# Probability codes as bytes in fp16's 1024, with the 1024 taken off by the matrix engine

## Chip, cores and metric

One NeuronCore of a Trainium2 chip runs the whole program in one launch. The metric is the device time of one execution in microseconds; the time before is the median of three runs.

## What is computed

Four transformer blocks in a row on x [4, 512, 128] with a context [4, 154, 128], 16 heads of 8 in the first three. Only the third block's two attentions, which are fake-quantised, are touched here. One is self-attention (512 keys), one cross-attention (154 keys):

```python
def _fq(x, delta, zp, n_bits):
    xi = _round_ste(x / delta) + zp
    xq = jnp.clip(xi, 0.0, 2.0 ** n_bits - 1.0)
    return (xq - zp) * delta

sim = jnp.einsum('bhid,bhjd->bhij', _fq(q, dq, 128.0, 8), _fq(k, dk, 128.0, 8)) * SCALE
attn = jax.nn.softmax(sim, axis=-1)
out = jnp.einsum('bhij,bhjd->bhid', _fq(attn, dw, 0.0, 8), _fq(v, dv, 128.0, 8))
```

The probabilities become integer codes from 0 to 255 (probability / dw, rounded, clipped), the values integer codes from -128 to 127, and the products of codes are summed exactly.

## The kernel before, in words

Each engine runs a program of its own, written out by hand in the order of a table of items, and the engines meet at semaphores. A unit is one attention of one sequence; units 16 to 19 are the quantised self-attentions of the four sequences, 20 to 23 the cross-attentions. A unit is cut into steps: in self-attention 32, each of one tile of 128 queries with 2 heads and 512 keys; in cross-attention 16, each of one tile with 4 heads and 154 keys. That makes 192 steps. Two steps are a pair, 96 in all.

A step i goes through the engines like this (names as in the code):

- PE, `scores_quant(i)` (L1280): products of query and key codes into one of three double banks (`score0`, `score1`, `trans`); it waits until ACT is done with the bank's earlier step i-3.
- DVE, L2064: the largest score of every row (`top_score`). Ahead of it in DVE's loop stands the reciprocal L2058 of the row sums of step i-2 (in cross-attention L2057 scales them first).
- ACT, L1572 scales the tops, L1581 takes exp into `probs` (three slots) with the row sum `total`.
- POOL, L2278 (self-attention only) multiplies two reciprocals by 1/dw; L2289 makes the codes: probability times reciprocal plus 1024.0 (`HALF_ROUND`), written as fp16. Between 1024 and 2048 fp16 holds just the integers, so the write rounds. It is 2 instructions of 512 columns in a self-attention step and 4 of 154 in a cross-attention step, into `codes` (four slots).
- SP, L926: a DMA transpose of the step's [128, 1024] fp16 codes into `pT_raised` (eight slots).
- DVE, `copy_codes` (L2047): takes 1024 off, cuts at 255 and writes bf16 `pT_codes`; it runs `QUANT_LAG` = 6 steps behind DVE's top. `pT_codes` and `pT_raised` are one place in SBUF.
- PE, `weigh_pair(n)` (L1299): 16 products of value codes and probability codes, four of them in each of PE's column groups, summed into `acc`; it runs `WEIGH_LAG` = 8 steps behind.

After a unit's last pair DVE scales `acc` into `oT` (L2072). Among the steps the items of the neighbouring units run: output product and statistics (W), normalisation (M), transposed features (H), and the next unit's Q, K and V with their rounding on DVE. In units 16 and 17 POOL also issues 16 gathers of expert rows (L2235). Ahead of the stage stands the expert stage, whose last products end with semaphore `down_raised`; its buffers share SBUF with `codes`.

Elsewhere in the kernel, and used below as rows only: L2182, a POOL cast of 154 columns; L2188, a POOL multiplication of 154 bf16 columns by one column (`term_row`), with no second operation; L2189, a POOL sum of two bf16 operands; L2244, a POOL memset; L1246, the experts' down products.

Of the kernel before, what the change touches and what calls it, by code (L numbers as in the profile page):

```python
# [14 lines left out]
ROUND = 1.5 * 2.0 ** 23  # L15
HALF_ROUND = 1024.0
LOWEST = -1.0e30
# [5 lines left out]
CODE_SOURCES = 4  # L23
QUANT_LAG, WEIGH_LAG, GROUPED_LAG = 6, 8, 2

# [377 lines left out]
def build(nc, io, out):  # L403
# [3 lines left out]
    with ctx:  # L407
# [143 lines left out]
        put = place(arena, quant_at)  # L551
        k_codes = put([P, 2, TOKENS], bf16)
        quant_at = [16384]
        put = place(arena, quant_at)
        qT_codes, k4_codes = put([P, 2, TOKENS], bf16), put([P, 2, 4, TOKENS], bf16)

        v_quant, v_quant_tail = put([P, 2, TILES, HEADS, 32], bf16), put([P, 2, HEADS, 32], bf16)
        probs = put([P, 3, 2, TOKENS])
        pT_at = quant_at[0]
        pT_codes = put([P, CODE_SLOTS, 2 * TILES, P], bf16)  # L560
        put = place(arena, [pT_at])
        pT_raised = put([P, CODE_SLOTS, 2 * TILES, P], fp16)
        put = place(arena, [0])
        codes = put([P, CODE_SOURCES, 2, TOKENS], fp16)
        put = place(arena, quant_at)
        q_round, k_round, v_round = put([P, TOKENS]), put([P, TOKENS]), put([P, TILES, D])
# [108 lines left out]
        codes_ready = sem("codes_ready")  # L675
        codes_copied = sem("codes_copied")
        pair_weighed = sem("pair_weighed")
# [116 lines left out]
        with nc.Block() as block:  # L794

            @block.sync
            def _(sp):
# [122 lines left out]
                for i in range(len(QUANT_STEPS)):  # L920
                    if i in KEYS_AFTER:
                        copy_keys(KEYS_AFTER[i])
                    sp.wait_ge(codes_ready, i + 1)
                    if i >= CODE_SLOTS:
                        sp.wait_ge(pair_weighed, (i - CODE_SLOTS) // 2 + 1)
                    sp.dma_start_transpose(pT_raised[:, i % CODE_SLOTS, :, :],  # L926
                                           codes[:, i % CODE_SOURCES, :, :].rearrange("p j k -> p (j k)"))\
                        .then_inc(codes_turned[i % CODE_SLOTS], 16)
# [22 lines left out]
            def _(pe):  # L951
# [333 lines left out]
                def weigh_pair(n):  # L1285

                    u, t, _, first, heads = quant_step(2 * n)
                    pe.wait_ge(codes_copied, 2 * n + 2)
                    if 2 * n == QUANT_BASE[u]:
                        pe.wait_ge(v_coded, u - 15)  # L1290
                        if u > 16:
                            pe.wait_ge(oT_ready, u - 16)
                    tiles = 2 if is_cross(u) else TILES
                    for z in range(heads):
                        i = first + z
                        for k in range(tiles):
                            vals = v_quant_tail[:, u % 2, :, :] if is_cross(u) and k else v_quant[:, u % 2, k, :, :]
                            for j in range(4):
                                ins = nc.tensor.matmul(acc[32 * j:32 * j + 32, P * t:P * (t + 1)], vals[:, 4 * j + i, :],  # L1299
                                                       pT_codes[:, (2 * n + j // 2) % CODE_SLOTS, j % 2 * TILES + tiles * z + k, :],  # L1300
                                                       start=(i == 0 and k == 0), stop=(i == 3 and k == tiles - 1))
                    ins.then_inc(pair_weighed, 1)
# [41 lines left out]

                pe.wait_ge(codes_copied, len(QUANT_STEPS))
                pe.wait_ge(quant_exp, len(QUANT_STEPS))
# [295 lines left out]
            def _(dve):  # L1642
# [399 lines left out]

                def copy_codes(i):

                    of = i % CODE_SLOTS
                    dve.wait_ge(codes_turned[of], 16 * (i // CODE_SLOTS + 1))
                    nc.vector.tensor_scalar(pT_codes[:, of, :, :].rearrange("p k q -> p (k q)"),  # L2047
                                            pT_raised[:, of, :, :].rearrange("p k q -> p (k q)"),
                                            -HALF_ROUND, 255.0, ALU.add, ALU.min).then_inc(codes_copied, 1)

                quant_steps = len(QUANT_STEPS)
                for i in range(quant_steps + WEIGH_LAG + 2):
# [6 lines left out]
                    if i < quant_steps:  # L2059
                        src = quant_score[i % 3][:, :, :]  # L2060
                        if is_cross(QUANT_STEPS[i][0]):
# [3 lines left out]
                                                negate=True).then_inc(quant_top, 1)  # L2065
                    if QUANT_LAG <= i < quant_steps + QUANT_LAG:
                        copy_codes(i - QUANT_LAG)
                    if i in QUANT_LAST:
# [75 lines left out]
            def _(pool):  # L2144
# [121 lines left out]
                def of_step(z, i):  # L2266
                    u, t, a, h, heads = quant_step(i)
                    z = z[:, :].rearrange("p (t x j i) -> p t x j i", x=2, j=2, i=4)[:, t, a, :, h:h + heads]
                    return z if heads > 1 else z.rearrange("p j i -> p (j i)")

                quant_steps = len(QUANT_STEPS)
                for i in range(quant_steps + 1):
                    if i:
# [9 lines left out]
                        for j in range(2):  # L2283
                            for z in range(heads):
# [3 lines left out]
                                to = slice(z * 2 * P, z * 2 * P + width)  # L2288
                                ins = nc.gpsimd.tensor_scalar(codes[:, (i - 1) % CODE_SOURCES, j, to], probs[:, (i - 1) % 3, j, of],  # L2289
                                                              inv_total[:, at_col:at_col + 1], HALF_ROUND, ALU.mult, ALU.add)  # L2290
                        ins.then_inc(codes_ready, 1)
# [99 lines left out]
```

## Time and profile before

| | |
|---|---|
| median of 3 runs | 1576.75 us (1573.37 to 1578.98) |
| the profiled execution | 1576.92 us |
| its span | 1575.1 us |
| mean granted clock of PE | 0.826 |
| PE busy | 1092.8 us |
| DVE busy | 1098.1 us |
| ACT busy | 894.2 us |
| POOL busy | 681.1 us |

Busy times are sums over the whole span. The quantised stage begins at about 685 us and ends at about 1167 us. A "wait" is idle time of an engine put down to what released it; a clock of 0.50 is the lower of PE's two levels, 1.2 GHz.

### The profile page before, as it was taken

The page shows a single profiled execution, that of the slowest core. Times are in us where ns is not written, and L with a number is a line of the kernel's source. Part 1 is how long each engine was busy: PE and PEld are TensorE (multiplying, and loading weights), DVE is VectorE, ACT ScalarE, POOL GpSimd, SP SyncE. Part 2 cuts the span into 40 slices and gives each one's busy share as a digit, 9 for nine tenths or more (in the row PEclk, how much of TensorE's full clock was granted, in tenths as well). Part 3 has the DMA queues.
Part 4 walks back from the last instruction along what each step waited for, and adds up shares of the span by engine and source line. Part 5 has one row for each costly group of instructions (what it writes and reads, how often), then busy time and mean ns, then how long its engine had stood idle before and what let it go on. Part 6 is the DMA issues. An engine that isn't in the chain of part 4 may idle for free.

```text
span 1575.1 us, 28607 instructions
## 1 busy us (share of the span) xinstructions
PE 1092.8 (69%) x9344; PEld 593.3 (38%) x9344; DVE 1098.1 (70%) x3102; ACT 894.2 (57%) x2546; POOL 681.1 (43%) x1055
## 2 busy tenths in 40 slices
PE   2888888887788797855353545444358778888888
PEld 1333344444333286831120212222225435453545
DVE  2687777777688653678888999877765666666522
ACT  1555554555554464567676797988852344646531
POOL 3321011011011416558888888877741344445310
PEclk9899999999999998975555555555569799999989
DMA  5213142101331112267555576665530121201000
GB/s 184 61 53 92 51 129 75 54 24 50 99 106 49 42 39 82 57 160 122 99 104 109 106 130 115 121 109 106 109 57 14 27 48 35 49 21 43 1 0 27
DMA packets 265219, 116.53 MB, mean 74 GB/s; under 512 B 216936, under 2 KB 253936, under 8 KB 262896
## 3 DMA queue, kind: packets, MB, share of 16 engines
q1 hardware_dynamic: 260112, 108.29, 30.8%
q0 software_dynamic: 2048, 4.20, 0.9%
q10 hardware_dynamic: 2912, 2.22, 0.5%
q8 instruction: 75, 1.23, 0.3%
q14 instruction: 72, 0.59, 0.1%
HBM read 38.80 MB, written 16.45 MB: 35 GB/s over the span
## 4 chain that ended last, share of the span: by engine, by line
PE 35%; POOL 21%; DVE 18%; issue 14%; ACT 9%; DMA 1%; SPq 0%; POOLq 0%; another core or an unknown queue 0%; ACTq 0%; DVEq 0%
POOL arena L2289 12%; ACT arena L1581 4%; PE acc L1199 3%; POOL inv_total L2278 2%; PE trans L1171 2%; DVE minus_top L1980 2%; PE misc L1021 2%; PE misc L1027 2%; PE trans L1323 2%; ACT arena L1528 2%; PE score L1335 2%; PE score L1337 2%; PE trans L1177 1%; POOL arena L2235 1%; PE acc L1385 1%
## 5 line engine op out<-in xcount | busy, mean ns | idle before, releaser
L2289 POOL TENSOR_SCALAR arena<-arena,inv_total 128x512 f16<-128x512 f32 (+1 forms) x512 | 299.7, 585 | 57.3 <-DVE inv_total L2058 16.8
L1980 DVE TENSOR_REDUCE minus_top<-score 128x4 f32<-128x616 f32 (+4 forms) x256 | 200.6, 802 | 95.3 <-PE score L1141 36.9
L2154 POOL TENSOR_TENSOR rstd<-spread,minus_half 128x4 f32<-128x4 f32 x36 | 37.5, 1043 | 489.5 <-DVE spread L1662 414.0
L1581 ACT ACTIVATE arena<-score,minus_top,exp_scale 128x512 f32<-128x512 f32 (+1 forms) x340 | 210.4, 625 | 20.9 <-POOL arena L2289 11.9
L1528 ACT ACTIVATE arena<-trans 128x512 f32<-128x512 f32 x240 | 134.4, 596 | 109.3 <-PE trans L1177 104.0
L1619 ACT ACTIVATE arena<-arena,minus_top 128x154 f32<-128x154 f32 x256 | 105.2, 412 | 129.3 <-DVE minus_top L2123 129.1
L1280 PE MATMUL score<-arena 32*128 32x512 bf16 (+1 forms) x340 | 68.9, 458 | 139.7 <-ACT arena L1581 138.7
L2064 DVE TENSOR_REDUCE top_score<-score 128x2 f32<-128x1024 f32 (+1 forms) x128 | 135.7, 1061 | 0.6 <-PE score L1280 0.5
L2309 POOL TENSOR_TENSOR arena<-arena,inv_total 128x512 f32<-128x512 f32 x64 | 66.5, 1040 | 143.9 <-DVE inv_total L2131 130.0
L1581 ACT ACTIVATE arena<-trans,minus_top,exp_scale 128x154 f32<-128x154 f32 (+1 forms) x172 | 105.5, 620 | 19.2 <-POOL arena L2289 14.9
L2118 DVE CUSTOM_DVE_ANT_0 arena<-score,arena 128x154 f32<-128x154 f32 x256 | 65.9, 313 | 60.6 <-PE score L1360 60.2
L2047 DVE TENSOR_SCALAR arena<-arena 128x1024 bf16<-128x1024 f16 x192 | 103.1, 537 | 5.9 <-DMA arena<-arena 5.9
L1572 ACT ACTIVATE minus_top<-top_score,exp_scale 128x2 f32<-128x2 f32 (+1 forms) x192 | 56.4, 294 | 52.9 <-DVE top_score L2064 52.4
L1280 PEld LDWEIGHTS score<-arena 32*128 32x128 bf16 x340 | 14.2, 102 | 191.0 <-ACT arena L1581 173.9
L1280 PE MATMUL trans<-arena 32*128 32x154 bf16 (+1 forms) x172 | 34.9, 454 | 72.8 <-ACT arena L1581 72.8
L1199 PE MATMUL acc<-arena 128*32 128x512 f32 (+3 forms) x768 | 79.9, 504 | 4.7 <-issue 4.0
L1299 PE MATMUL acc<-arena 128*32 128x128 bf16 x1536 | 59.3, 307 | 27.9 <-DVE oT L2072 15.3
L1546 ACT ACTIVATE arena<-score,arena 128x128 f32<-128x128 f32 x184 | 52.0, 370 | 44.2 <-PE score L1236 38.1
L1528 ACT ACTIVATE arena<-trans,arena 128x512 f32<-128x512 f32 x80 | 52.2, 686 | 28.5 <-PE trans L1177 27.3
L2064 DVE TENSOR_REDUCE top_score<-trans 128x2 f32<-128x1024 f32 (+1 forms) x64 | 67.4, 1053 | 0.0
L1581 ACT ACTIVATION_READ_ACCUMULATOR arena<-score,minus_top,exp_scale 128x1 f32 x340 | 66.6, 196 | 0.0
L1177 PE MATMUL trans<-arena 64*128 64x512 bf16 (+3 forms) x384 | 63.3, 327 | 0.0
(283 smaller groups left out, 2814.4 us busy)
## 6 DMA issues: line engine op xcount, KB each, us to landing
arena<-q_terms SPq DMA_DIRECT2D x88, 128.0 KB, 2.8
late<-arena SPq DMA_DIRECT2D x128, 64.0 KB, 2.0
q_terms<-arena SPq DMA_DIRECT2D x36, 128.0 KB
late<-k_terms SPq DMA_DIRECT2D x32, 128.0 KB, 3.1
arena<-arena SPq DMA_TRANSPOSE x192, 3.1
by_expert<-zeros SPq DMA_DIRECT2D x2, 1472.0 KB, 9.8
arena<-by_expert SPq DMA_DIRECT2D x10, 256.0 KB
from_expert<-arena SPq DMA_DIRECT2D x10, 256.0 KB
```

Source lines behind the costliest of these rows:

```text
L1177: ins = nc.tensor.matmul(to, ones[r, j, :], top_rows[r, g % 2, q0:TOKENS], start=False, stop=True)
L1199: ins = nc.tensor.matmul(acc[32 * j:32 * j + 32, q0:TOKENS], v_cols[:, k, 4 * g + j, :], src, start=(b % half == 0 and k == 0), stop=(last ...
L1280: ins = nc.tensor.matmul(quant_score[i % 3][:, j, z * n:(z + 1) * n], qT_codes[r:r + 32, u % 2, t * P:(t + 1) * P], k4_codes[r:r + 32, u % ...
L1528: nc.scalar.activation(expT[w % SLOTS], trans[w % 2][:, :], ACT.Exp, bias=bias)\
L1581: ins = nc.scalar.activation(probs[:, i % 3, j, of], quant_score[i % 3][:, j, of], ACT.Exp, bias=minus_top[:, at_col:at_col + 1], scale=ex ...
L1619: ins = nc.scalar.activation(gq_exp_p[:, i % 3, h, :], shifted[:, i % 3, h, :], ACT.Exp, bias=minus_top[:, at_col:at_col + 1], accum_out=t ...
L1980: nc.vector.tensor_reduce(dst, src, axis=AX.X, op=ALU.max, negate=True).then_inc(top_ready, 1)
L2047: nc.vector.tensor_scalar(pT_codes[:, of, :, :].rearrange("p k q -> p (k q)"), pT_raised[:, of, :, :].rearrange("p k q -> p (k q)"), -HALF ...
L2064: nc.vector.tensor_reduce(of_step(top_score, i), src, axis=AX.X, op=ALU.max, negate=True).then_inc(quant_top, 1)
L2118: ins = nc.vector.tensor_tensor_reduce(out=shifted[:, i % 3, h, :], in0=score[i % 2][:, odd, z * CTX:(z + 1) * CTX], in1=mask_add[:, b % 2 ...
L2289: ins = nc.gpsimd.tensor_scalar(codes[:, (i - 1) % CODE_SOURCES, j, to], probs[:, (i - 1) % 3, j, of], inv_total[:, at_col:at_col + 1], HA ...
L2309: nc.gpsimd.tensor_tensor(gq_p[:, v % 2, :, :], gq_exp_p[:, v % 3, :, 0:P], inv.to_broadcast([P, 4, P]), ALU.mult)
```

## The change

`codes` is filled once with 1024.0, and a constant tile `minus_base` of -1024.0 is made. POOL's L2289 now only multiplies, and writes its result as unsigned bytes into the low byte of each fp16 code, so that the fp16 reads 1024 + code. The DMA transpose writes straight into `pT_codes`, which is fp16 now, as are the value codes. DVE's `copy_codes` is gone. PE's `weigh_pair` waits for the transposes, and follows each four products by four more of the same values with `minus_base`, which take off 1024 times the values' sum. Semaphore `codes_set` takes the place of `codes_copied`.

```diff
-        v_quant, v_quant_tail = put([P, 2, TILES, HEADS, 32], bf16), put([P, 2, HEADS, 32], bf16)
+        v_quant, v_quant_tail = put([P, 2, TILES, HEADS, 32], fp16), put([P, 2, HEADS, 32], fp16)
...
+        pT_codes = put([P, CODE_SLOTS, 2 * TILES, P], fp16)
         put = place(arena, [0])
+
         codes = put([P, CODE_SOURCES, 2, TOKENS], fp16)
+        code_bytes = codes.rearrange("p i j k -> p (i j k)").bitcast(mybir.dt.uint8)
+        code_bytes = code_bytes.rearrange("p (i j k b) -> p i j k b", i=CODE_SOURCES, j=2, b=2)[:, :, :, :, 0]
...
                 def weigh_pair(n):
 
                     u, t, _, first, heads = quant_step(2 * n)
-                    pe.wait_ge(codes_copied, 2 * n + 2)
+                    for i in (2 * n, 2 * n + 1):
+                        pe.wait_ge(codes_turned[i % CODE_SLOTS], 16 * (i // CODE_SLOTS + 1))
...
                             for j in range(4):
-                                ins = nc.tensor.matmul(acc[32 * j:32 * j + 32, P * t:P * (t + 1)], vals[:, 4 * j + i, :],
-                                                       pT_codes[:, (2 * n + j // 2) % CODE_SLOTS, j % 2 * TILES + tiles * z + k, :],
-                                                       start=(i == 0 and k == 0), stop=(i == 3 and k == tiles - 1))
+                                nc.tensor.matmul(acc[32 * j:32 * j + 32, P * t:P * (t + 1)], vals[:, 4 * j + i, :],
+                                                 pT_codes[:, (2 * n + j // 2) % CODE_SLOTS, j % 2 * TILES + tiles * z + k, :],
+                                                 start=(i == 0 and k == 0), stop=False)
+                            for j in range(4):
+                                ins = nc.tensor.matmul(acc[32 * j:32 * j + 32, P * t:P * (t + 1)], vals[:, 4 * j + i, :], minus_base,
+                                                       start=False, stop=(i == 3 and k == tiles - 1))
...
-                def copy_codes(i):
-
-                    of = i % CODE_SLOTS
-                    dve.wait_ge(codes_turned[of], 16 * (i // CODE_SLOTS + 1))
-                    nc.vector.tensor_scalar(pT_codes[:, of, :, :].rearrange("p k q -> p (k q)"),
-                                            pT_raised[:, of, :, :].rearrange("p k q -> p (k q)"),
-                                            -HALF_ROUND, 255.0, ALU.add, ALU.min).then_inc(codes_copied, 1)
...
+                pool.wait_ge(down_raised, ALL_BLOCKS)
+                nc.gpsimd.memset(codes.rearrange("p i j k -> p (i j k)"), CODE_BASE).then_inc(codes_set, 1)
+                nc.gpsimd.memset(minus_base, -CODE_BASE).then_inc(codes_set, 1)
+                pool.wait_ge(codes_set, 2)
...
-                                ins = nc.gpsimd.tensor_scalar(codes[:, (i - 1) % CODE_SOURCES, j, to], probs[:, (i - 1) % 3, j, of],
-                                                              inv_total[:, at_col:at_col + 1], HALF_ROUND, ALU.mult, ALU.add)
+
+                                ins = nc.gpsimd.tensor_scalar(code_bytes[:, (i - 1) % CODE_SOURCES, j, to], probs[:, (i - 1) % 3, j, of],
+                                                              inv_total[:, at_col:at_col + 1], None, ALU.mult)
```

On DVE, in the middle of unit 16, the order before was this (L2047 the copy, L2058 the reciprocal, L2064 the tops):

```order
L2058 RECIPROCAL inv_total<-total 128x2
L2064 TENSOR_REDUCE top_score<-score1 128x2
L2047 TENSOR_SCALAR arena<-arena 128x1024
L2058 RECIPROCAL inv_total<-total 128x2
L2064 TENSOR_REDUCE top_score<-trans 128x2
```

and is now this (L2053 and L2059 are the same two lines of the changed file):

```order
L2053 RECIPROCAL inv_total<-total 128x2
L2059 TENSOR_REDUCE top_score<-score0 128x2
L2053 RECIPROCAL inv_total<-total 128x2
L2059 TENSOR_REDUCE top_score<-score1 128x2
L2053 RECIPROCAL inv_total<-total 128x2
```

The third instruction of every step has gone; nothing else on DVE changes place.

On POOL, where the stage begins, the order is now this (L2276 and L2288 are the lines that were L2278 and L2289):

```order
L2151 TENSOR_TENSOR x<-x,rows 128x512
L2266 MEMSET arena 128x4096
L2267 MEMSET arena 128x128
L2276 TENSOR_SCALAR inv_total<-inv_total,inv_sizes 128x2
L2288 TENSOR_SCALAR arena<-arena,inv_total 128x512 x2
```

The two fills stand between the expert stage's last item and the first step's multiplication; before, the multiplication followed directly.

On PE a pair was one row, sixteen L1299 between the scores of two steps:

```order
L1280 MATMUL trans<-arena 128x512 x2
L1280 MATMUL score<-arena 128x512 x2
L1299 MATMUL acc<-arena 32x128 x16
L1280 MATMUL score<-arena 128x512 x2
L1280 MATMUL trans<-arena 128x512 x2
```

and begins now like this, with the two rows of four repeated four times for each pair:

```order
L1280 MATMUL trans<-arena 128x512 x2
L1280 MATMUL score<-arena 128x512 x2
L1300 MATMUL acc<-arena 32x128 x4
L1304 MATMUL acc<-arena 32x128 x4
L1300 MATMUL acc<-arena 32x128 x4
```

The scores keep their place; a pair has 32 matmuls where it had 16.

## Rows read from the trace of the kernel before

**Rows 1.** The page, busy us (share of the span), instructions.

```profile
PE 1092.8 (69%) x9344; PEld 593.3 (38%) x9344; DVE 1098.1 (70%) x3102; ACT 894.2 (57%) x2546; POOL 681.1 (43%) x1055
```

**Rows 2.** Busy time by unit; columns in the first row; units 17 and 21.

```profile
core 0: us, PE busy (x) PEld busy (x) DVE busy (x) ACT busy (x) POOL busy (x), PEclk, DMA share, GB/s
...
788.00:875.00 87.00, 37.48 (x348) 14.90 (x348) 75.92 (x158) 61.40 (x166) 74.53 (x114) 0.50 0.58 107
...
1059.00:1099.00 40.00, 18.36 (x212) 9.12 (x212) 31.05 (x98) 35.06 (x145) 30.92 (x67) 0.50 0.55 106
```

**Rows 3.** Timeline of POOL at the stage's start (start, duration, then idle before).

```profile
690.56 0.31 POOL L2278 TENSOR_SCALAR inv_total<-inv_total,inv_sizes 128x2 f32<-128x2 f32 x1 [8.97 <-DVE inv_total L2058]
...
692.51 0.29 POOL L2278 TENSOR_SCALAR inv_total<-inv_total,inv_sizes 128x2 f32<-128x2 f32 x1
...
694.44 0.29 POOL L2278 TENSOR_SCALAR inv_total<-inv_total,inv_sizes 128x2 f32<-128x2 f32 x1
```

**Rows 4.** Timeline of POOL, later in self-attention.

```profile
922.08 0.34 POOL L2278 TENSOR_SCALAR inv_total<-inv_total,inv_sizes 128x2 f32<-128x2 f32 x1
...
924.07 0.34 POOL L2278 TENSOR_SCALAR inv_total<-inv_total,inv_sizes 128x2 f32<-128x2 f32 x1
```

**Rows 5.** Timeline of all engines at the same place.

```profile
920.58 1.21 DVE L2064 TENSOR_REDUCE top_score<-score 128x2 f32<-128x1024 f32 x1
920.74 0.78 ACT L1581 ACTIVATE arena<-trans,minus_top,exp_scale 128x512 f32<-128x512 f32 x1
...
921.05 0.62 PE L1299 MATMUL acc<-arena 128*32 128x128 bf16 x16
...
922.64 0.78 ACT L1581 ACTIVATE arena<-score,minus_top,exp_scale 128x512 f32<-128x512 f32 x1
...
923.60 0.65 DVE L2047 TENSOR_SCALAR arena<-arena 128x1024 bf16<-128x1024 f16 x1
```

**Rows 6.** Waits from 700 to 1167: us in total, times, longest us.

```profile
PE score L1280 <- ACT arena L1581: 130.5, 88, 5.2
...
ACT minus_top L1572 <- DVE top_score L2064: 49.8, 35, 3.8
...
ACT arena L1581 <- POOL arena L2289: 26.8, 48, 1.6
...
POOL arena L2289 <- DVE inv_total L2058: 16.8, 21, 2.6
POOL inv_total L2278 <- DVE inv_total L2058: 11.4, 11, 2.1
```

**Rows 7.** DVE's groups, 690 to 1170: busy us, mean ns, idle before.

```profile
L2047 DVE TENSOR_SCALAR arena<-arena 128x1024 bf16<-128x1024 f16 x192 | 103.1, 537 | 5.9 <-DMA arena<-arena 5.9
```

**Rows 8.** POOL's groups over the span, by shape.

```profile
L2289 POOL TENSOR_SCALAR arena<-arena,inv_total 128x512 f16<-128x512 f32 x256 | 184.6, 721 | 22.4 <-DMA arena<-arena 1.1
L2289 POOL TENSOR_SCALAR arena<-arena,inv_total 128x154 f16<-128x154 f32 x256 | 115.1, 450 | 34.9 <-DVE inv_total L2058 16.8
...
L2278 POOL TENSOR_SCALAR inv_total<-inv_total,inv_sizes 128x2 f32<-128x2 f32 x128 | 43.2, 338 | 29.4 <-DVE inv_total L2058 20.3
...
L2188 POOL TENSOR_SCALAR arena<-arena,term_row 128x154 bf16<-128x154 bf16 x12 | 8.3, 691 | 1.2
...
L2244 POOL MEMSET arena<- 128x2048 f32 x1 | 1.8, 1818 | 0.0
...
L2189 POOL TENSOR_TENSOR arena<-arena 128x154 bf16<-128x154 bf16 x4 | 1.8, 444 | 0.3
...
L2182 POOL CAST arena<-arena 128x154 bf16<-128x154 f32 x4 | 1.2, 312 | 0.3
```

**Rows 9.** Single lines: ns min/median/max, starts; L2289 before 699 only.

```profile
L2188 POOL TENSOR_SCALAR arena<-arena,term_row x12: 674/675/817, 12.7 to 112.2; 128x154 bf16<-128x154 bf16 x12
...
L2289 POOL TENSOR_SCALAR arena<-arena,inv_total x8: 692/692/692, 691.0 to 697.5; 128x512 f16<-128x512 f32 x8
```

**Rows 10.** The chain of waits: start, us, what; the last expert.

```profile
683.50 1.07 PE trans L1246 x8
```

More of the change, by code:

```diff
@@ L15 @@
 ROUND = 1.5 * 2.0 ** 23
-HALF_ROUND = 1024.0
+CODE_BASE = 1024.0
 LOWEST = -1.0e30
@@ L23 @@
 CODE_SOURCES = 4
-QUANT_LAG, WEIGH_LAG, GROUPED_LAG = 6, 8, 2
+WEIGH_LAG, GROUPED_LAG = 8, 2
 PAIR_TILES = 2 * TILES
@@ L551, in build @@
         put = place(arena, quant_at)
-        k_codes = put([P, 2, TOKENS], bf16)
+        k_codes, minus_base = put([P, 2, TOKENS], bf16), put([P, P], fp16)
         quant_at = [16384]
@@ L555, in build @@
         qT_codes, k4_codes = put([P, 2, TOKENS], bf16), put([P, 2, 4, TOKENS], bf16)
-        v_quant, v_quant_tail = put([P, 2, TILES, HEADS, 32], bf16), put([P, 2, HEADS, 32], bf16)
+        v_quant, v_quant_tail = put([P, 2, TILES, HEADS, 32], fp16), put([P, 2, HEADS, 32], fp16)
         probs = put([P, 3, 2, TOKENS])
[L559 to L562, printed above, removed]
+        pT_codes = put([P, CODE_SLOTS, 2 * TILES, P], fp16)
         put = place(arena, [0])
         codes = put([P, CODE_SOURCES, 2, TOKENS], fp16)
+        code_bytes = codes.rearrange("p i j k -> p (i j k)").bitcast(mybir.dt.uint8)
+        code_bytes = code_bytes.rearrange("p (i j k b) -> p i j k b", i=CODE_SOURCES, j=2, b=2)[:, :, :, :, 0]
         put = place(arena, quant_at)
@@ L675, in build @@
         codes_ready = sem("codes_ready")
-        codes_copied = sem("codes_copied")
+        codes_set = sem("codes_set")
         pair_weighed = sem("pair_weighed")
@@ L925, in _ @@
                         sp.wait_ge(pair_weighed, (i - CODE_SLOTS) // 2 + 1)
-                    sp.dma_start_transpose(pT_raised[:, i % CODE_SLOTS, :, :],
+                    sp.dma_start_transpose(pT_codes[:, i % CODE_SLOTS, :, :],
                                            codes[:, i % CODE_SOURCES, :, :].rearrange("p j k -> p (j k)"))\
@@ L1343, in feed_forward @@
                     downs(B - 1)
-                pe.wait_ge(codes_copied, len(QUANT_STEPS))
                 pe.wait_ge(quant_exp, len(QUANT_STEPS))
@@ L2065, in _ @@
                                                 negate=True).then_inc(quant_top, 1)
-                    if QUANT_LAG <= i < quant_steps + QUANT_LAG:
-                        copy_codes(i - QUANT_LAG)
                     if i in QUANT_LAST:
```

## The prediction

> **What bounds the kernel now.** The page's busy shares come first [rows 1]: the busiest, DVE, works 70% of the span, and the average over stages says little: the stage of the change has to be read alone. That is the two quantised attentions, units 16 to 23, from 690.5 to 1166.7 us of the span. Its busy time by unit [rows 2] shows how near three engines are to their limit: in unit 17, self-attention, DVE works 75.92, ACT 61.40 and POOL 74.53 of 87.00 us; in unit 21, cross, ACT leads with 35.06 of 40.00. PE works under half the time, at a granted clock of 0.50 (its lower level, 1.2 GHz).
>
> Which of the three ends last is read from the timeline of POOL. In the first steps, before the first L2047 runs on DVE, a POOL step repeats every 1.95 and 1.93 us: 690.56, 692.51, 694.44 [rows 3]. Later it starts at 922.08 and 924.07, 1.99 us apart [rows 4], while ACT's steps start at 920.74 and 922.64, 1.90 apart [rows 5]. POOL is the slowest by 4%, ACT is next, and DVE (1.21 for the top and 0.65 for L2047 alone [rows 5]) has no slack to catch up when the Q, K, V and normalisation items come between. The waits confirm both [rows 6]: ACT waits 26.8 us for POOL's L2289 and 49.8 us for DVE's tops; POOL waits 16.8 + 11.4 us for DVE's reciprocals. PE's long waits are for ACT, 130.5 us on the score banks: it has spare time.
>
> **Removed from DVE.** 192 copies L2047, 103.1 us [rows 7]: 0.54 us a step. It lies on no bound directly; it pays in two ways.
> (a) POOL runs freer. With L2047 present L2289 takes 721 ns in the mean over the 256 wide ones and L2278 338 [rows 8]; before the first L2047 they take 692 and 290 [rows 9, 3]. 256 x 0.029 + 128 x 0.048 = 7.4 + 6.1 = 13.5 us, all in self-attention and all on the bound.
> (b) POOL's 28.2 us of waiting for DVE [rows 6]. DVE gains 0.5 us a step to catch up, but the items themselves stay. Between none and all, I take half, 14 us: item work is larger than L2047 at any one place, yet L2047 is what keeps DVE late in the steps after it.
> The Trainium skill (SBUF — State Buffer, section "Who interferes with whom") says that a VectorE instruction in a 2-port mode, as a tensor_scalar within SBUF can be, blocks GpSimd fully. By that rule the 128 copies of the self-attentions, 0.54 us each, would have blocked POOL for up to 69 us. The rows show 13.5, so most copies must fall where POOL doesn't ask for the ports, or give way themselves; the sum goes by the rows.
>
> **Changed on POOL.** 512 L2289, each now one multiplication to bytes at every second place instead of a multiplication and an addition to fp16. No row shows a byte output. Lower bound: the 154-column cast L2182, 312 ns against 450 of the 154-column L2289 [rows 8], so 138 ns less. POOL would drop well under ACT, whose 1.90 us against POOL's 1.93 would bound: 128 x 0.03 = 4 us more gain in self-attention, and the other half of POOL's waits, 14 us. Upper bound: L2188, the only other POOL operation that multiplies by a column and does nothing else: 691 ns for 154 columns (median 675 [rows 9]), half again as much as L2289, with bf16 in and out. I take no change, from the row nearest in input, width and column scalar: L2289 itself. Why not L2188: its input is 16 bits wide, as the new one's is not. But the row speaks against the change and carries the main rival.
>
> **Start on POOL.** Two memsets, of 4096 and 128 fp16 columns, after the last expert. 2048 f32 columns take 1818 ns [rows 8]: by bytes the large one would take 1.8 us, by columns 3.64. I take 3.64, and under 0.3 for the small one. The last expert's L1246 ends at about 684.56, so they run from 684.7 to 688.7; POOL's first step starts at 690.56 after 8.97 us idle [rows 10, 3]. They cost nothing, with 1.9 us to spare; without that cover, 4 us once.
>
> **Added on PE.** 16 more matmuls a pair on the same operand shapes, with their weight loads. 16 take 0.62 us from the first start to the last end [rows 5], so 96 x 0.62 = 59.5 us of PE time at the low clock. The cover is PE's waiting for ACT, 130.5 us over the stage on the score banks alone [rows 6]; with three banks scores are also issued a step before DVE reads them, so 0.62 us of lateness every second step does not reach DVE. Where it isn't covered is the end of a unit: last pair, oT, output product. PE now waits for the transpose itself and not for the copy behind it, 0.54 us, so 0.1 net a unit; with PE's items near by I take +2 us in all. Bounds: 0 and 30 (half uncovered).
>
> **DMA** moves the same bytes in transposes of the same shape; only the place they land in has another type. Cost nothing.
>
> **Sum** against the profiled execution's 1576.9 us (span 1575.1; the median of the runs is 1576.75, the same): -13.5 - 14 + 2 = -25.5, rounded to **1552 us.** A measurement of this kernel tells from no change about 0.3%, 4.7 us; 25 is well beyond that.
>
> **Rivals.**
> *B, slower: the one-operation byte form is slow on POOL.* L2188's excess over L2289 is 0.225 us on 154 columns (675 against 450). In proportion to columns that is 0.748 on 512. Self-attention: 256 x 0.748 = 191.5 us; cross: 256 x 0.225 = 57.6. POOL is then the bound everywhere, so its waits and contention are swallowed: 191.5 + 57.6 - 28.2 - 13.5 = +207.4, **1784 us**; read as slope over a fixed 0.29 (0.385 us for 152 columns), the wide one would take 1.58 us, the excess 0.89, and the time 1821. For it: L2188 takes 674 to 817 ns in all 12 places, so it is no collision; and bf16 alone is slow neither as input (L2189, a sum of two bf16 operands, 444 ns) nor as output (L2182) [rows 8, 9]. Against: two stages of arithmetic being cheaper than one needs a path made for just that pair; L2278, also one multiplication, is as cheap as it can be, but has two columns. It turns the sign already when the wide form costs over 0.1 us more: 256 x 0.1 = 26 us.
> The Trainium skill (GPSIMD Engine Reference, sections 3.1 and 4.1) speaks for the forecast: it calls one-input work roughly line-rate and bound by the port up to two operations an element; by it the new form would cost what the old one did, and the forecast stands as it is. L2188 doesn't fit that rule.
>
> *C, PE's additions show.* If half of the 59.5 us lands on the path (scores late behind the longer pair, then tops, then ACT), -27.5 + 30 = +2.5: **1579 us**, no change. For: at the end of a unit PE items and the pair stand in a row. Against: 130.5 us of waiting for ACT.
>
> *D, ACT bounds.* POOL's byte form is cheaper, as the cast's row allows, and DVE's lateness vanishes with its copies: ACT's 1.90 us a step and none of POOL's 28 us of waits: -13.5 - 28 - 4 + 2 = -43.5, **1533 us**. For: ACT has the longest steady busy time in cross units [rows 2]. Against: DVE's items are still there.
>
> *E, the change doesn't do what it says*: the slowdown of L2289 isn't from L2047, POOL stays at 1.99 and only DVE frees itself: -14 + 2, **1565 us**. Still faster.
>
> **How the numbers follow.** Forecast (with E) 0.48, D 0.08, C 0.08, B 0.36. The gain needs one thing only, an unchanged L2289, and the one row that is like its new form speaks against; hence 0.36 and no less. Faster by over 0.3% 0.56, within 0.3% 0.08, slower 0.36. The forecast's own range is 1538 to 1567. The range of all reaches from 1535 over C to 1800, which takes in B in proportion and leaves out its steeper form and D.
>
> **What would show it.** In the profile after: no DVE line for copies, DVE near 64% of the span ((1098.1 - 103.1)/1552); the POOL group of codes at 690 ns (forecast) or over 1.3 us (B) for 512 columns; the small POOL multiplication back at 290 ns; a POOL step of 1.93 us; ACT's wait for DVE's tops well under 49.8 us; POOL's memset over by 688.6; a pair's 32 matmuls in 1.24 us at clock 0.50. I am wrong if codes cost over 0.1 us more, if PE's matmuls of pairs become what DVE's tops wait for, or if POOL steps in 1.93 us and the stage is no shorter.

## Result: 12.6% slower, and the profile after

The changed kernel takes 1775.06 us in the median of 4 runs (1763.69 to 1780.65), the kernel before 1575.06 in the runs beside it (4 runs). The ratio is 1.126, 95% interval 1.119 to 1.133: slower by some 200 us. The forecast of 1552 was wrong, rival B (1784) was what happened, and the time lies inside the range of all, 1535 to 1800. The profiled execution took 1763.69 us, its span is 1761.9.

The page's busy row of the kernel after answers to [rows 1]:

```profile
PE 1125.5 (64%) x10880; PEld 630.4 (36%) x10880; DVE 1024.9 (58%) x2910; ACT 893.0 (51%) x2546; POOL 946.9 (54%) x1057
```

DVE lost 73 us, ACT none; POOL gained 266. (DVE's 73 are less than the copies' 103.1 for two reasons: a copy started some 0.09 us before the top ahead of it ended, which the page counts once, 192 x 0.09 = 17 us; and DVE's other instructions in the stage got longer by 13 us in sum, 7.2 of them in L2052, the scaling of the cross-attentions.) Where POOL gained them is in its groups by shape (lines moved: L2289 is now L2288, L2278 is L2276), beside [rows 8]:

```profile
L2288 POOL TENSOR_SCALAR arena<-arena,inv_total 128x512 uint8<-128x512 f32 x256 | 399.8, 1574 | 11.9
L2288 POOL TENSOR_SCALAR arena<-arena,inv_total 128x154 uint8<-128x154 f32 x256 | 169.8, 703 | 0.4
...
L2276 POOL TENSOR_SCALAR inv_total<-inv_total,inv_sizes 128x2 f32<-128x2 f32 x128 | 39.5, 309 | 3.6 <-DVE inv_total L2053 2.2
```

A multiplication that used to take 721 ns takes 1574, the short one 703 instead of 450. POOL's waits for DVE have shrunk to almost nothing. The timeline of POOL at the stage's start, with the two fills, answers to [rows 3]:

```profile
685.44 3.51 POOL L2266 MEMSET arena<- 128x4096 f16 x1 [3.09 <-PE trans L1246]
688.89 0.21 POOL L2267 MEMSET arena<- 128x128 f16 x1
...
694.82 0.30 POOL L2276 TENSOR_SCALAR inv_total<-inv_total,inv_sizes 128x2 f32<-128x2 f32 x1
695.22 3.11 POOL L2288 TENSOR_SCALAR arena<-arena,inv_total 128x512 uint8<-128x512 f32 x2
698.29 0.30 POOL L2276 TENSOR_SCALAR inv_total<-inv_total,inv_sizes 128x2 f32<-128x2 f32 x1
```

The fills are over at 689.1, before the first step needs POOL. A step then repeats every 3.47 us instead of 1.93. The waits from 700 to 1362 say who stands behind POOL, beside [rows 6]:

```profile
ACT arena L1584 <- POOL arena L2288: 250.9, 173, 3.2
PE score L1280 <- ACT arena L1584: 229.8, 99, 5.6
DVE inv_total L2053 <- ACT arena L1584: 204.4, 94, 3.5
...
ACT minus_top L1575 <- DVE top_score L2059: 30.7, 18, 3.7
```

The order of these is a chain: ACT waits 250.9 us (26.8 before) because `probs` has three slots and POOL has not read the oldest; PE and DVE wait for ACT. POOL alone waits for nobody. The busy time of the stage adds up; these are the windows before (684.5 to 1167) and after (685 to 1362):

```profile
684.50:1167.00 482.50, 211.70 (x2210) 89.35 (x2210) 401.36 (x923) 382.18 (x1227) 387.88 (x680) 0.51 0.63 117
```

```profile
685.00:1362.00 677.00, 252.33 (x3748) 129.70 (x3748) 328.24 (x731) 380.51 (x1228) 653.44 (x682) 0.52 0.44 84
```

POOL (the fifth engine of the row) worked 387.9 of 482.5 us and now works 653.4 of 677.0. Its work rose by 265.6, its idle time fell from 94.6 to 23.6, by 71.0: 265.6 - 71.0 = 194.6 us, the 194.5 by which the stage is longer. All of the loss is there and is POOL's.

### The profile page after: what moved, and what is told of

Same layout as the page of the kernel before. It is cut to its first block, busy times and chain, and to the rows that moved or that the text cites. A ratio compares the mean times of both kernels' runs of the same rounds, so it can differ in the third digit from the quotient of the medians.

```text
span 1761.9 us, 31585 instructions
## 1 busy us (share of the span) xinstructions
PE 1125.5 (64%) x10880; PEld 630.4 (36%) x10880; DVE 1024.9 (58%) x2910; ACT 893.0 (51%) x2546; POOL 946.9 (54%) x1057
## 4 chain that ended last, share of the span: by engine, by line
POOL 37%; PE 30%; DVE 14%; issue 12%; ACT 5%; DMA 1%; SPq 0%; POOLq 0%; DVEq 0%; ACTq 0%
POOL arena L2288 28%; PE acc L1199 2%; DVE minus_top L1983 2%; POOL inv_total L2276 2%; PE trans L1171 2%; PE misc L1021 2%; PE misc L1027 2%; PE trans L1327 2%; ACT arena L1531 2%; PE score L1339 1%; PE score L1341 1%; DVE arena L1749 1%; PE trans L1177 1%; POOL arena L2228 1%; PE score L1236 1%
## 5 line engine op out<-in xcount | busy, mean ns | idle before, releaser
L2288 POOL TENSOR_SCALAR arena<-arena,inv_total 128x512 uint8<-128x512 f32 (+1 forms) x512 | 569.5, 1139 | 12.3
L2053 DVE RECIPROCAL inv_total<-total 128x2 f32<-128x2 f32 (+1 forms) x192 | 32.8, 171 | 210.6 <-ACT arena L1584 208.3
L2059 DVE TENSOR_REDUCE top_score<-score 128x2 f32<-128x1024 f32 (+1 forms) x128 | 135.8, 1062 | 1.6 <-PE score L1280 1.6
L1300 PE MATMUL acc<-arena 128*32 128x128 f16 x1536 | 89.3, 306 | 25.1 <-DMA arena<-arena 13.3
L1304 PE MATMUL acc<-arena 128*32 128x128 f16 x1536 | 91.9, 312 | 0.0
L1300 PEld LDWEIGHTS acc<-arena 128*32 128x32 f16 x1536 | 54.3, 137 | 59.3 <-issue 59.1
L2059 DVE TENSOR_REDUCE top_score<-trans 128x2 f32<-128x1024 f32 (+1 forms) x64 | 67.5, 1055 | 0.5 <-PE trans L1280 0.5
L1531 ACT ACTIVATE arena<-trans,arena 128x512 f32<-128x512 f32 x80 | 52.3, 687 | 28.7 <-PE trans L1177 27.5
```

Of the source, the lines that this page charges most:

```text
L1531: nc.scalar.activation(expT[w % SLOTS], trans[w % 2][:, :], ACT.Exp, bias=bias)\
L2059: nc.vector.tensor_reduce(of_step(top_score, i), src, axis=AX.X, op=ALU.max, negate=True).then_inc(quant_top, 1)
L2288: ins = nc.gpsimd.tensor_scalar(code_bytes[:, (i - 1) % CODE_SOURCES, j, to], probs[:, (i - 1) % 3, j, of], inv_total[:, at_col:at_col + 1 ...
```

## The experiments

What in L2288 is slow? Three things about it are new: the byte output, its stride of two bytes, and the missing second operation. Theory 1 says it is the missing operation, theory 2 the bytes or their stride. Four kernels put this question and price PE's added products; four more divide the gain that is left once L2288 is mended.

Executions of one kernel differ by up to 19 us, and in the profiled ones much of that arises ahead of the stage: the first reciprocal starts anywhere from 690.2 to 705.1 us, behind code that no edit touches but e8's, and that in 12 short instructions. So two measures stand in this table: the ratio of whole times, with its interval, and the stage of the one profiled execution, from the first start of the reciprocal (L2058, now L2053) to the start of the last `oT` (L2072, now L2065).

| kernel | median us (runs) | ratio to before | stage us |
|---|---|---|---|
| before | 1576.75 (3) | | 690.2 to 1166.7: 476.5 |
| after | 1775.06 (4) | 1.126 [1.119, 1.133] | 691.0 to 1361.7: 670.7 |
| e1_two_ops_bytes | 1561.97 (4) | 0.988 [0.983, 0.993] | 705.1 to 1157.8: 452.7 |
| e2_one_op_fp16 | 1805.54 (1) | one execution, none taken | 700.5 to 1396.9: 696.4 |
| e4_pe_only | 1585.20 (10) | 1.004 [1.001, 1.007] | 692.8 to 1173.5: 480.7 |
| e5_no_take_off | 1558.93 (6) | 0.985 [0.981, 0.990] | 697.5 to 1147.3: 449.8 |
| e6_copy_back | 1579.14 (12) | 0.998 [0.995, 1.001] | 698.3 to 1170.1: 471.8 |
| e7_scale_in_second_op | 1548.14 (6) | 0.978 [0.975, 0.981] | 701.9 to 1145.1: 443.2 |
| e8_pads_two_ops | 1541.02 (5) | 0.980 [0.977, 0.982] | 692.0 to 1135.3: 443.3 |

The kernel before took 1582.4 to 1582.6 in the median beside e1 to e7, and 1576.5 beside e8; the ratios take that into account. How well the stage of one execution repeats is known from one pair only: e7 and e8 run the same instructions in it and took 443.2 and 443.3 us.

**e1_two_ops_bytes**: the changed kernel, with a second operation that does nothing.

```diff
-    inv_total[:, at_col:at_col + 1], None, ALU.mult)
+    inv_total[:, at_col:at_col + 1], 0.0, ALU.mult, ALU.add)
```

> The changed kernel with one word more: POOL's L2288 multiplies and adds 0.0, into the same bytes. Theory 1 (a tensor_scalar with a column and no second operation is slow on POOL, whatever it writes): L2288 falls from 1574 to about 690 ns (512 columns) and from 703 to about 450 ns (154), a POOL step of 1.93 us, and the whole to the forecast's 1552 us (1538 to 1567), faster than both kernels. Theory 2 (writing bytes at every second place is slow): L2288 stays near 1574 and 703 ns, the time near 1775 us. Theory 3 (both have a part): in between, about 1650 us.

Measured: ratio 0.988, where the change itself gave 1.126. POOL's groups in the stage:

```profile
L2288 POOL TENSOR_SCALAR arena<-arena,inv_total 128x512 uint8<-128x512 f32 x256 | 176.4, 702 | 14.2 <-DMA arena<-arena 2.3
L2288 POOL TENSOR_SCALAR arena<-arena,inv_total 128x154 uint8<-128x154 f32 x256 | 97.7, 406 | 50.6 <-DVE inv_total L2053 50.2
L2276 POOL TENSOR_SCALAR inv_total<-inv_total,inv_sizes 128x2 f32<-128x2 f32 x128 | 38.0, 297 | 28.7 <-DVE inv_total L2053 26.9
```

Adding 0.0 takes the instruction from 1574 to 702 ns, to the same byte places. The same change, with two operations, is faster than the kernel before.

**e2_one_op_fp16**: the other way round, the kernel before with its addition left out. The codes then lack the 1024, so the copies take off what isn't there and the attention sums are something else.

```diff
-    inv_total[:, at_col:at_col + 1], HALF_ROUND, ALU.mult, ALU.add)
+    inv_total[:, at_col:at_col + 1], None, ALU.mult)
```

> The kernel before with the addition of 1024 left out of L2289 (so the codes are not raised, and the copy on DVE takes 1024 off nothing: the quantised attentions compute something else). Theory 1: L2289 rises from 721 to about 1570 ns and from 450 to about 700, the time to about 1780 us. Theory 2: L2289 stays at 721 and 450 ns, and the time at 1575 us. Theory 3: in between.

POOL's groups, with no byte anywhere:

```profile
L2289 POOL TENSOR_SCALAR arena<-arena,inv_total 128x512 f16<-128x512 f32 x256 | 408.7, 1607 | 12.0
L2289 POOL TENSOR_SCALAR arena<-arena,inv_total 128x154 f16<-128x154 f32 x256 | 180.7, 725 | 0.4
```

The whole loss comes back without the rest of the change (1805.54 us in the one execution, where about 1780 was expected; DVE's copies are still there). Theory 2 has fallen.

**e3_pool_forms**: e1 with 57 POOL instructions behind the fills, on the experts' idle buffer, each form four times on 512 columns. They lengthen the kernel, to 1617.77 us in one execution, and touch nothing it reads.

```diff
+    for _ in range(4):
+        then(nc.gpsimd.tensor_scalar(h_out, f_in, col_s, 1024.0, ALU.mult, ALU.add))
+    for _ in range(4):
+        then(nc.gpsimd.tensor_scalar(h_out, f_in, col_s, None, ALU.mult))
...
```

> The two-operation byte kernel with 57 POOL instructions put behind the two fills, four of each form, each waiting for the one before, 512 columns each: multiplication by a column alone or with an addition, into fp16, f32, bytes side by side and bytes at every second place, bf16 to bf16, and with a number in place of the column, also two multiplications, and a cast to bytes. Theory 1: each form with one operation takes about 1.5 us and each with two 0.7, for every type. Theory 2: fp16 and f32 outputs take 0.7 us with either, byte outputs 1.5 us; if the stride matters, only the spread ones. A third possibility, that only a column as operand with one operation is slow, shows in the forms with a number. The time of the whole says nothing here: all engines wait for these instructions, some 60 us.

The forms by type, column as scalar (L2280 one operation with fp16 out, L2278 two; L2282 and L2284 the same with f32 out; L2286 bytes, one, L2288 two; L2290 bytes at every second place, one, L2292 two; L2294 bf16 in and out, one, L2296 two), then with a number in place of the column (L2298 one, L2300 two), and a cast:

```profile
L2280 POOL TENSOR_SCALAR arena<-arena,inv_sizes 128x512 f16<-128x512 f32 x4 | 6.3, 1566 | 0.4
...
L2290 POOL TENSOR_SCALAR arena<-arena,inv_sizes 128x512 uint8<-128x512 f32 x4 | 6.3, 1564 | 0.4
L2286 POOL TENSOR_SCALAR arena<-arena,inv_sizes 128x512 uint8<-128x512 f32 x4 | 6.2, 1562 | 0.4
L2282 POOL TENSOR_SCALAR arena<-arena,inv_sizes 128x512 f32<-128x512 f32 x4 | 6.2, 1562 | 0.4
L2294 POOL TENSOR_SCALAR arena<-arena,inv_sizes 128x512 bf16<-128x512 bf16 x4 | 6.2, 1562 | 0.4
L2298 POOL TENSOR_SCALAR arena<-arena 128x512 f16<-128x512 f32 x4 | 5.9, 1487 | 0.3
...
L2292 POOL TENSOR_SCALAR arena<-arena,inv_sizes 128x512 uint8<-128x512 f32 x4 | 2.8, 695 | 0.4
L2288 POOL TENSOR_SCALAR arena<-arena,inv_sizes 128x512 uint8<-128x512 f32 x4 | 2.8, 692 | 0.4
L2278 POOL TENSOR_SCALAR arena<-arena,inv_sizes 128x512 f16<-128x512 f32 x4 | 2.8, 692 | 0.4
L2284 POOL TENSOR_SCALAR arena<-arena,inv_sizes 128x512 f32<-128x512 f32 x4 | 2.8, 692 | 0.4
L2296 POOL TENSOR_SCALAR arena<-arena,inv_sizes 128x512 bf16<-128x512 bf16 x4 | 2.8, 692 | 0.4
...
L2300 POOL TENSOR_SCALAR arena<-arena 128x512 f16<-128x512 f32 x4 | 2.5, 617 | 0.3
L2304 POOL CAST arena<-arena 128x512 uint8<-128x512 f32 x4 | 2.4, 612 | 0.3
```

One operation costs 1562 to 1566 ns and two cost 692 to 695, whatever the types and the stride: 2.26 times as much. With a number it is 1487 against 617. The types, the bytes and the stride are worth 4 ns at most. The first operation is a multiplication in every form tried.

**e4_pe_only**: the kernel before with PE's added products alone, against a tile of zeros (`no_base`, bf16, filled once by POOL). The diff shows the added products.

```diff
+    for j in range(4):
+        ins = nc.tensor.matmul(acc[32 * j:32 * j + 32, P * t:P * (t + 1)], vals[:, 4 * j + i, :], no_base,
+                               start=False, stop=(i == 3 and k == tiles - 1))
```

> The kernel before with the 16 further products a pair added, by a tile of zeros in place of -1024, and nothing else changed (POOL fills the tile once). If PE's added 59.5 us lie under its waits for ACT, as I argued: no change, 1575 to 1580 us. If half of it shows (rival C): 1600 us or more.

Ratio 1.004, 6 us (1.7 to 10.4), and 4.2 us in the stage: small, though not the none that was expected. PE's wait for ACT covers nearly all of the added products. Rival C, which had half of them on the path, falls.

**e5_no_take_off**: e1 without the products with `minus_base`; the 1024s stay in the sums, so this kernel leaves the taking off out. The diff shows the products that are gone.

```diff
-    for j in range(4):
-        ins = nc.tensor.matmul(acc[32 * j:32 * j + 32, P * t:P * (t + 1)], vals[:, 4 * j + i, :], minus_base,
-                               start=False, stop=(i == 3 and k == tiles - 1))
```

> e1_two_ops_bytes without the products with minus_base: the 1024s stay in the sums, so the output is not the reference's. It prices PE's 96 x 0.62 = 59.5 us in the place where they stand, with DVE's copies gone. Theory (the waits for ACT cover them, as e4_pe_only showed on the kernel before, +6 us of 59.5): 2 to 8 us faster than e1_two_ops_bytes' ratio gives, ratio to the kernel before 0.983 to 0.987. Rival C in part (with DVE and POOL quicker, the longer pair is what delays the scores, and it ate what DVE's copies gave): 12 us or more faster than e1_two_ops_bytes, ratio 0.980 or less.

The ratio is 0.985 against e1's 0.988; their intervals overlap, so the runs don't tell them apart: by the ratios alone the difference could be anything from none to 14 us. The stage is 2.9 us shorter. It is the stage that puts the products' price in place at a few us, and the 12 of the rival didn't appear in it.

**e6_copy_back**: e1 with DVE's 192 copies put back into a tile that nobody reads, PE waiting for them (the lines that place the tile are not shown).

```diff
+    def copy_codes(i):
+        of = i % CODE_SLOTS
+        if i:
+            dve.wait_ge(codes_copied, i)
+        dve.wait_ge(codes_turned[of], 16 * (i // CODE_SLOTS + 1))
+        nc.vector.tensor_scalar(copied.rearrange("p k q -> p (k q)"), pT_codes[:, of, :, :].rearrange("p k q -> p (k q)"),
+                                -CODE_BASE, 255.0, ALU.add, ALU.min).then_inc(codes_copied, 1)
...
-    for i in (2 * n, 2 * n + 1):
-        pe.wait_ge(codes_turned[i % CODE_SLOTS], 16 * (i // CODE_SLOTS + 1))
+    pe.wait_ge(codes_copied, 2 * n + 2)
```

> e1_two_ops_bytes with DVE's copies put back, 192 of 512 columns as before, into a scratch tile that nobody reads, and PE waiting for the copy as before; the products with minus_base stay. Theory (the gain is DVE's: contention on POOL 13.5 us, and POOL's and ACT's waits for DVE): L2288 back from 702 to about 720 ns, the small POOL multiplication from 297 to about 338, and the time at the kernel before plus what PE adds, ratio 0.998 to 1.008. Rival (the gain comes from POOL's side, byte output or the two operations' form, or from PE not waiting for a copy): ratio at or under 0.993.

Ratio 0.998 (0.995 to 1.001): most of e1's gain goes; the stage is 19.1 us longer than e1's. So most of the gain is the copies', but not all of it. e6 has PE's added products as e4 has, and DVE's copies as well, and its stage is 8.9 us shorter than e4's (471.8 against 480.7; the ratios, 0.998 and 1.004, say the same). POOL's step is 1.89 us here with a copy in it (925.15 to 927.04), and was 1.99 before [rows 4]; what made it shorter is taken up below, under POOL's step. The timeline of DVE and then of POOL in mid-stage shows both engines paying (L2053 is the copy, L2301 the codes):

```profile
925.75 0.75 DVE L2053 TENSOR_SCALAR arena<-arena 128x1024 bf16<-128x1024 f16 x1
...
927.66 0.74 DVE L2053 TENSOR_SCALAR arena<-arena 128x1024 bf16<-128x1024 f16 x1
```

```profile
925.15 0.29 POOL L2289 TENSOR_SCALAR inv_total<-inv_total,inv_sizes 128x2 f32<-128x2 f32 x1
925.53 1.53 POOL L2301 TENSOR_SCALAR arena<-arena,inv_total 128x512 uint8<-128x512 f32 x2
927.04 0.29 POOL L2289 TENSOR_SCALAR inv_total<-inv_total,inv_sizes 128x2 f32<-128x2 f32 x1
```

The pair of codes takes 1.53 us beside a copy and 1.36 in e1, and the copy 0.75 (0.54 in the mean of [rows 7], but 0.42 in the median and 0.40 at the least, so about 0.42 where POOL leaves it alone):

```profile
L2047 DVE TENSOR_SCALAR arena<-arena x192: 395/424/1070, 699.6 to 1165.5; 128x1024 bf16<-128x1024 f16 x192
```

In the means of the groups the codes go from 702 to 757 ns (wide) and 406 to 447 (narrow), the small multiplication from 297 to 325: 256 x 0.055 + 256 x 0.041 + 128 x 0.028 = 28 us of POOL's work, where the forecast had 13.5. For the wide codes 720 ns were expected here, not 757.

**e7_scale_in_second_op**: e1 with work for the second operation. The scale goes into it, so POOL's small multiplication (L2276, in self-attention) and DVE's (L2052, in cross-attention) fall away.

```diff
-    then(nc.vector.tensor_scalar(t, t, sizes[:, 7:8], None, ALU.mult))
...
-    then(nc.gpsimd.tensor_scalar(of_step(inv_total, i - 1), of_step(inv_total, i - 1),
-                                 inv_sizes[:, 3:4], None, ALU.mult))
...
-    inv_total[:, at_col:at_col + 1], 0.0, ALU.mult, ALU.add)
+    inv_total[:, at_col:at_col + 1], inv_sizes[:, 7:8] if is_cross(u) else inv_sizes[:, 3:4], ALU.mult, ALU.mult)
```

> e1_two_ops_bytes with a use for the second operation: the codes are multiplied by the column 1/total and then by the column with the scale, so POOL's small multiplication of each self-attention step (297 ns) and DVE's of each cross step (L2052) fall away; the same values are computed. If POOL's step bounds the self-attentions: its step falls by 0.3 us to ACT's 1.90 at most, and half of POOL's 0.3 x 128 = 38 us shows, 8 to 20 us faster than e1_two_ops_bytes, ratio 0.975 to 0.983. If DVE with its items and ACT already bound there (POOL waits 77 us for DVE in e1_two_ops_bytes): under 5 us, ratio 0.985 to 0.988.

Ratio 0.978 (0.975 to 0.981), 15 us under e1 by the ratios, and the stage another 9.5 us shorter: the first of the two expectations. The codes' own rows are dearer, and POOL still has time left:

```profile
L2283 POOL TENSOR_SCALAR arena<-arena,inv_total,inv_sizes 128x512 uint8<-128x512 f32 x256 | 193.9, 769 | 54.6 <-DVE inv_total L2051 49.5 <-DMA arena<-arena 3.5
```

```profile
930.19 1.52 POOL L2283 TENSOR_SCALAR arena<-arena,inv_total,inv_sizes 128x512 uint8<-128x512 f32 x2 [0.38 <-DVE inv_total L2051]
932.10 1.52 POOL L2283 TENSOR_SCALAR arena<-arena,inv_total,inv_sizes 128x512 uint8<-128x512 f32 x2 [0.39 <-DVE inv_total L2051]
```

A second column costs 67 ns an instruction (769 against 702), 0.13 a step, and saves the small one's 0.30 and the gap of 0.10 behind it. POOL now idles 0.39 us of every 1.91. The starts of the eight `oT` divide the 9.5 us, since POOL's small multiplication stood only in the self-attentions and DVE's only in the cross-attentions: against e1 the four self-attentions are 7.2 us shorter (3.9, 2.5, 0.3 and 0.5), the four cross-attentions 2.3. So two thirds of the gain lie where POOL has the 16 gathers as well, in units 16 and 17; the steps of 1.91 us, the same in both kernels, give nothing.

**e8_pads_two_ops**: e7 with the same cure for the pads' multiplication, the row the prediction took for a warning (L2188 before, L2179 here).

```diff
-    pad_terms[:, t, :], pad_terms[:, t, :], term_row[:, t:t + 1], None, ALU.mult))
+    pad_terms[:, t, :], pad_terms[:, t, :], term_row[:, t:t + 1], 0.0, ALU.mult, ALU.add))
```

> e7_scale_in_second_op with the same cure for the row that the prediction read as a warning: POOL's 12 multiplications of the pad terms by a column (154 bf16 columns, median 674 ns) get an addition of 0.0 as second operation. Theory (any tensor_scalar on POOL without a second operation takes the slow form): from 674 to about 400 ns, near the 406 of the 154-column codes. Rival (bf16 or writing in place made that row slow): it stays at 674. The time: 12 x 0.27 = 3.3 us at most if POOL's pads were on a path, none if not; ratio 0.976 to 0.980.

The single line, to be read beside [rows 9]:

```profile
L2179 POOL TENSOR_SCALAR arena<-arena,term_row x12: 394/400/537, 12.8 to 111.2; 128x154 bf16<-128x154 bf16 x12
```

From a median of 675 ns to 400. That warning was the same effect, and nothing else. The time doesn't move (0.980 against 0.978, intervals overlapping; the stage 443.3 against 443.2): these 12 instructions are on no path. e7 and e8 are the fastest kernels of the study, about 33 us under the kernel before by their ratios.

## Why the prediction was wrong, and where it was right

**The step that failed** is "Changed on POOL ... I take no change, from the row nearest in input, width and column scalar". Nearness was judged by types and shape, and the types are worth 4 ns at most. What mattered was the form: how many operations the instruction carries. The one row of that form, L2188 at 675 ns for 154 columns [rows 9], was set aside because its input is bf16. e1 and e2 turn the effect off and on with that operand alone, e3 shows it for each type, and e8 cures L2188 itself. The argument against B, that two operations can't be cheaper than one without a path made for just that pair, is wrong: multiplication with addition and multiplication with multiplication (e7) are both fast. The runs don't show why. L2278, cheap with one operation, could say nothing on the question: by the prices per column worked out in the last section, its two columns carry 3 ns of the effect.

The rule of the Trainium skill (GPSIMD Engine Reference, sections 3.1 and 4.1) was weighed as speaking for the forecast: one-input work bound by the port up to two operations an element. By it the new form costs what the old did. The runs show 1562 against 692 ns, so for one operation without a second it doesn't hold here; the measurement decides.

**Rival B** gave 1784 for a measured 1775, by two errors that nearly cancel. Its operations were too small: 191.5 + 57.6 = 249.1 us against the groups' (399.8 - 184.6) + (169.8 - 115.1) = 269.9. Its cover was too small as well: 28.2 of waits and 13.5 of contention make 41.7, where POOL's idle time fell by 71.0 (the contention is in the groups' growth already). The waits named for DVE were not all of POOL's idle time; the difference between a stage's length and an engine's work in it is. What the forecast left out are mostly gaps of some 0.07 us that followed nearly every codes instruction of the kernel before, 36.5 us in all over 466 of them in its trace, and that the changed kernel hasn't (more under POOL's step). Its steeper reading, L2188 as a slope over a fixed part, gave 1.58 us for the wide form: 1574 ns measured. It missed by 46 us, two thirds through the same small cover, one third through its operations: 256 x 0.89 + 57.6 = 285.4 for the measured 269.9.

**The rest of the forecast**, read in e1, which is the change with POOL's form mended. Forecast was -25.5 us; the ratio says -19 (-11 to -27), the stage -23.8. That it comes so near is in part luck: by the stages it is +4.2 for PE (e4), -8.9 for what byte codes with 0.0 changed besides (e6 against e4; the gaps that POOL loses, below, are the likely part), which the forecast didn't have, and -19.1 for the copies (e1 against e6), where it had -27.5. By unit, from the starts of `oT`, 16.1 of the 23.8 us are in units 16 and 17, where POOL also issues the gathers, 3.5 in units 18 and 19, and 4.2 in the cross-attentions.
- *(a) Contention, 13.5 us, all in self-attention.* Too small and not only there: e6 against e1 gives 28 us of POOL's work, 10.5 of it in the narrow codes of cross-attention. The rows of e6 show both engines stretched, 0.17 us for POOL's pair and 0.33 for the copy. The copy starts 0.22 us into the pair; had it waited for the first code instruction's 0.69 us to end and then taken its own 0.42, it would have ended at 926.64, and it ended at 926.50.
  The Trainium skill (SBUF — State Buffer, "Who interferes with whom") has one engine blocked fully by the other, whichever issued first. The rows come near that, with the copy giving way first; they don't prove it, and they don't speak against it. Of the forecast's two ways out for its 69 us, that copies miss POOL's work or give way themselves, the second is seen here.
- *(b) Half of POOL's 28.2 us of waits for DVE.* Wrong in kind. In e1 POOL waits 50.2 + 26.9 us for DVE's reciprocals, more than before, since it has become faster than what feeds it. The waits of e1 in the stage, and under them its timeline at 932 us:

```profile
POOL arena L2288 <- DVE inv_total L2053: 50.2, 51, 3.4
...
ACT minus_top L1575 <- DVE top_score L2059: 45.2, 29, 3.4
POOL inv_total L2276 <- DVE inv_total L2053: 26.9, 45, 3.6
```

```profile
932.21 0.78 ACT L1584 ACTIVATE arena<-score,minus_top,exp_scale 128x512 f32<-128x512 f32 x1
932.23 0.29 POOL L2276 TENSOR_SCALAR inv_total<-inv_total,inv_sizes 128x2 f32<-128x2 f32 x1 [0.16 <-DVE inv_total L2053]
...
933.87 0.17 DVE L2053 RECIPROCAL inv_total<-total 128x2 f32<-128x2 f32 x1 [0.62 <-ACT arena L1584]
...
934.12 0.78 ACT L1584 ACTIVATE arena<-score,minus_top,exp_scale 128x512 f32<-128x512 f32 x1
934.14 0.29 POOL L2276 TENSOR_SCALAR inv_total<-inv_total,inv_sizes 128x2 f32<-128x2 f32 x1 [0.16 <-DVE inv_total L2053]
```

  Here ACT starts a step every 1.91 us and waits for nobody; DVE waits 0.62 for ACT, and POOL 0.16 for DVE. That is rival D's bound, "ACT's 1.90 us a step". D's 1533 didn't come with it, since ACT still waits 45.2 us for DVE's tops where items stand between, against 49.8 before, and 6.7 for POOL's codes, against 26.8: DVE's items, not its copies, make most of that wait. And most of the gain was to be had in units 16 and 17, where POOL's gathers come on top of its steps. "ACT's wait well under 49.8" was wrong too.
- *POOL's step of 1.93 us* was taken as what its instructions need. In e1 it is 1.75 where nothing holds it (705.45 to 707.20): with the same 692 to 702 ns an instruction, the pair takes 1.36 us from start to end, where it took 1.46 before. The kernel before, e1 and e2, each in its first steps:

```profile
690.96 1.46 POOL L2289 TENSOR_SCALAR arena<-arena,inv_total 128x512 f16<-128x512 f32 x2
```

```profile
705.85 1.36 POOL L2288 TENSOR_SCALAR arena<-arena,inv_total 128x512 uint8<-128x512 f32 x2
707.20 0.29 POOL L2276 TENSOR_SCALAR inv_total<-inv_total,inv_sizes 128x2 f32<-128x2 f32 x1
```

```profile
701.27 3.12 POOL L2289 TENSOR_SCALAR arena<-arena,inv_total 128x512 f16<-128x512 f32 x2
```

  Twice 0.692 is 1.38, so 0.07 us stood between the two and about as much behind them; e1's two leave none. e2's two, which write fp16 too, leave none either (twice 1.564 is 3.13), nor do e7's with two multiplications (1.52 for twice 0.769). So fp16 output alone doesn't make the gap. It comes with the addition of 1024.0 into fp16; whether by the number or by fp16 output with a second operation wasn't tried. A codes instruction is 0.10 us dearer by it from start to start. Two in a step make 0.20 us, and by that POOL's step in e6 can be shorter than before with the copies in place. That these gaps are the whole of the 8.9 us between e4 and e6 is not shown.
- *PE, 59.5 us of work, 2 of it shown.* Right in kind: e4 shows 4 to 6 us, e5 about 3. The work was oversized. 32 matmuls take 1.04 us from first start (960.36) to last end in the changed kernel, where 1.24 was predicted; 0.62 for 16 holds a fixed part that a longer chain pays once, so it is 96 x 0.42 = 40 us, and PE's busy time in the stage rose by 40.6 (211.70 to 252.33 in the windows above).
- *Fills*: right, 3.51 and 0.21 us for 3.64 and under 0.3, hidden.
- *C and E* fell: e4 shows C's addition isn't on the path, and POOL's step and its instructions do get faster without the copies.

Of the forecast's signs, the copies' absence and the hidden fills came true in the changed kernel; "codes at 690 ns or over 1.3 us (B)" was the one that decided, and decided for B.

## What to carry to other kernels

When no row shows the new instruction, look for a row of its form (how many operations, which kinds of scalar) before one of its types: here the single row of the right form, on 154 columns, was right, and the rows alike in types and shape were not. On GpSimd (POOL) give a `tensor_scalar` that only multiplies a second operation: adding 0.0 took 1574 ns to 702; better, give it a factor that another instruction now applies. And size what a slower engine can swallow by its idle time in the stage, not by its named waits, and an instruction by its step from start to start, since a gap behind it can come or go with its form. When the engine gets faster instead, its waits grow, and the next engine's step is the floor.

## What the runs showed of the hardware that was not expected

- GpSimd's `tensor_scalar` with one operation, a multiplication: 1562 to 1566 ns on 512 columns with a column as scalar, 1487 with a number; with two operations 692 to 695 and 617; a cast 612. By columns (154 and 512): (1574 - 703) / 358 = 2.4 ns a column with one operation, (702 - 406) / 358 = 0.83 with two.
- It is the same within 4 ns for fp16, fp32, bf16 and bytes, contiguous or at every second byte (e3).
- A second column as operand in place of a number costs 67 ns on 512 columns and 76 on 154 (482 against 406), independent of width.
- A VectorE copy of 1024 columns and GpSimd's codes stretch each other: 0.75 us for the copy instead of about 0.42, 1.53 for the pair of codes instead of 1.36 (e6 against e1).
- Two GpSimd codes instructions behind one another, from start to end: 1.46 us for two of 692 ns with 1024.0 added into fp16 (the kernel before), 1.36 for two of about 700 with 0.0 added into bytes (e1).
